# The last two graphs of a four-layer graph network on one core: parts of the final elu moved from ACT to DVE

## The chip, the cores and the metric

The kernel runs on 1 core of one Trainium2 chip. The metric is the device time of the program on that core in microseconds (us), taken as the median over several runs; lower is better. TensorE is called PE here, VectorE DVE, ScalarE ACT, GpSimd POOL and SyncE SP. Times written as 281.12 or the like are microseconds from the start of the profiled span.

## The reference, cut to what matters

There are 32 graphs of 256 nodes with 128 features each. Four layers run one after another, each with a residual sum around it. In all of them the input of the layer is normalised and rectified first.

```python
h = jnp.maximum(_layernorm(x, axis=-1), 0.0)
x = x + _L0_gnn_ref(h, adj, L0_gnn_W, L0_gnn_a)               # attention
h = jnp.maximum(_layernorm(x, axis=-1), 0.0)
x = x + _L1_gnn_ref(h, adj, L1_gnn_a0, L1_gnn_a1, L1_gnn_a2, L1_gnn_a3)
h = jnp.maximum(_layernorm(x, axis=-1), 0.0)
x = x + _L2_gnn_ref(h, L2_gnn_adj, adj, L2_gnn_weight, L2_gnn_bias)
h = jnp.maximum(_layernorm(x, axis=-1), 0.0)
x = x + _L3_gnn_ref(h, adj, L3_gnn_W, L3_gnn_a)
```

The last layer is the one that matters here: it ends with `jax.nn.elu(attention @ Wh)`, and the output is `x + elu(y)`, where y is the attended sum of a node divided by its softmax sum, and elu(y) is y for y > 0 and exp(y) - 1 otherwise.

## The kernel before, in words

A unit is one layer of one graph: 4 x 32 = 128 units, numbered n = 0 to 127 by the list `ORDER` (lines 37 to 42). The second half of the graphs ends the list, so units 112 to 127 are layer 3 of graphs 16 to 31, in order. A graph has its 256 nodes as 128 partitions times T = 2 rows each, so a tile of features is 128x256 numbers, or two of 128x128.

Every engine runs its own hand-ordered software pipeline (`pipeline`, lines 79 to 84). A list names stages with a lag and the layers for which they run; in step s a stage with lag L handles unit s - L, and the stages of a step are issued in the order of the list. An engine issues in program order, and semaphores bind the engines. What sets the order at the end, for the units of layer 3:

- PE, `put_o` (lag 8, line 972): the attended sums of a unit into a PSUM bank (lines 998 and 1001). It waits for a bank of three that ACT has read (`y_ready`, line 977).
- DVE, `invert_sums` (lag 11, line 704): the softmax sums are bounded below (line 710) and inverted (line 712) into `rinv`.
- ACT, `elu_parts` (lag 9, line 560): for each of the two halves t it writes exp(y) into `expy` (line 567) and max(y, 0) into `relu_y` (line 568), both read from the PSUM bank with `rinv` as the scale, so 4 instructions a graph; the last signals `y_ready`.
- DVE, `elu` (lag 13, line 732): `expy` becomes min(exp(y), 1) + max(y, 0) in one instruction (line 736), which signals `elu_ready`. That is elu(y) + 1; the 1 has been taken off before, since the residual x in `x1` was made with `bias_less_1` (lines 364 and 395).
- The sum `result` = `expy` + `x1`: for even graphs on POOL in `add_x_even` (lag 13, line 399), for odd graphs on DVE in `add_x` (lag 15, line 739). Each signals its half of `result_ready`.
- SP, `store` (lag 13, line 322): waits for `result_ready` of the graph, then issues its DMA of 128 KB to `out`, in the order of the graphs.

In a step of DVE's list `add_x` stands ahead of `take_rows`, `invert_sums` and `elu` (lines 749 to 751). So the end of DVE's program, with units named by their graph, runs: add_x(27), invert_sums(31), elu(29), elu(30), add_x(29), elu(31), add_x(31), as the even graphs have no instruction in `add_x`.

After that DVE collects a flag that says whether a general fallback must run: lines 757 and 761, a matmul of PE (line 1011), and line 763. All engines load the flag and branch on it. SP does so only when its waits for the last stores are over (line 329), then waits for the flag (line 331) and loads it (line 332). The program ends when every engine has gone past that branch.

Of the kernel before, what the change touches and what calls it, by code (L numbers as in the profile page):

```python
# [8 lines left out]
B, N, D = 32, 256, 128  # L9
P = 128  # L10
T = N // P
# [12 lines left out]


SLOTS = 8
BEHIND = 2
EARLY = 3
HS = 12
XS = 12  # L30
WIDE = 16
ROUNDS = B // SLOTS

ALL, ATTEND, GATS, NORMED, MULTI_REL, RGCN_REL = (0, 1, 2, 3), (0, 1, 3), (0, 3), (1, 2), (1,), (2,)
NOT_LAST, FIRST, LAST = (0, 1, 2), (0,), (3,)
# [14 lines left out]
def nth(layers, n):  # L50

    return COUNTS[layers][n]
# [21 lines left out]
def gat_slot(n):  # L74

    return (nth(GATS, n) - 1) % SLOTS

# [22 lines left out]
def gat_stack(nc, x, adj, w0, a0, m0, m1, m2, m3, w2, b2, w3, a3, out):  # L100
    f32, bf16, i32, u32 = mybir.dt.float32, mybir.dt.bfloat16, mybir.dt.int32, mybir.dt.uint32
    ALU = mybir.AluOpType
    ACT = mybir.ActivationFunctionType
# [7 lines left out]
    with ctx:  # L111
# [3 lines left out]
        def sem(name):  # L115
            return ctx.enter_context(nc.semaphore(name))
# [18 lines left out]
        x1 = sb("x1", [P, WIDE, T, D])  # L135
        edges = sb("edges", [P, SLOTS, T, N], i32)
        absent = sb("absent", [P, WIDE, T, N], bf16)

        h = sb("h", [P, HS, T, 1 + D])
        xb = sb("xb", [P, SLOTS, T, D])  # L140
        result = sb("result", [P, SLOTS, T, D])
        st = sb("st", [P, WIDE, T, 9])
# [4 lines left out]
        rinv = sb("rinv", [P, WIDE, T])  # L147

        hT = sb("hT", [P, 4, N])
        haT = sb("haT", [P, 4, N])  # L150
        val = sb("val", [P, SLOTS, T, D + 3])
        edgesT = sb("edgesT", [P, WIDE, T, N])
# [5 lines left out]
        relu_y = sb("relu_y", [P, 4, T, D])  # L158
        expy = sb("expy", [P, 4, T, D])
# [59 lines left out]
        def bank_o(n):  # L219
            return bank[O_BANK[n]][:, 0:T * (1 + D)].rearrange("p (t c) -> p t c", t=T)  # L220
# [4 lines left out]
        stored = [sem(f"stored{k}") for k in range(SLOTS)]  # L225
# [32 lines left out]
        sums_ready = sem("sums_ready")  # L258
        rinv_ready = sem("rinv_ready")
        elu_ready = sem("elu_ready")  # L260
        o_taken = sem("o_taken")
        xb_ready = sem("xb_ready")
        bias_ready = sem("bias_ready")
        result_ready = [sem("result_ready_even"), sem("result_ready_odd")]
# [28 lines left out]
        @block.sync  # L293
        def _(sp):

            def load_first(k):
                sp.dma_start(edges[:, k].rearrange("p t n -> p (t n)"), adj_v[k]).then_inc(edges_loaded[k], 16)

            for k in range(XS):
                sp.dma_start(xin[:, k].rearrange("p t d -> p (t d)"), x_v[k]).then_inc(x_loaded[k], 16)  # L300
                if 1 <= k <= SLOTS:
                    load_first(k - 1)
                if k == 2:
                    sp.dma_start(w_gat[1][:, 0:D], w3).then_inc(gat_loaded[1], 16)
                    sp.dma_start(a_gat[1][:, :], a3.rearrange("(c p) o -> p (c o)", c=2), allow_slow_non_contiguous=True).then_inc(gat_loaded[1], 16)
            for r, m in enumerate((m0, m1, m2, m3)):
                sp.dma_start(a_rel[:, r:r + 1], m.rearrange("(p o) -> p o", o=1)).then_inc(loaded, 16)
            sp.dma_start(w_rel[:, :, :], w2.rearrange("r i o -> i r o")).then_inc(loaded, 16)
            sp.dma_start(bias[:, :], b2.rearrange("(o d) -> o d", o=1).to_broadcast([P, D])).then_inc(loaded, 16)

            def load_x(n, layer, g):
                if g + XS < B:
                    sp.wait_ge(o_taken, nth(NOT_LAST, n))
                    sp.dma_start(xin[:, g % XS].rearrange("p t d -> p (t d)"), x_v[g + XS]).then_inc(x_loaded[g % XS], 16)

            def load_edges(n, layer, g):
                k = g % SLOTS
                if g + SLOTS < B:
                    sp.wait_ge(absent_ready, nth(FIRST, n))
                    sp.dma_start(edges[:, k].rearrange("p t n -> p (t n)"), adj_v[g + SLOTS]).then_inc(edges_loaded[k], 16)  # L320

            def store(n, layer, g):
                k = g % SLOTS
                sp.wait_ge(result_ready[g % 2], (nth(LAST, n) + 1) // 2)
                sp.dma_start(out_v[g], result[:, k].rearrange("p t d -> p (t d)")).then_inc(stored[k], 16)

            pipeline([(load_x, SP_LAG, FIRST), (load_edges, SP_LAG, FIRST), (store, SP_LAG + 1, LAST)])
            for k in range(SLOTS):
                sp.wait_ge(stored[k], 16 * ROUNDS)

            sp.wait_ge(flag_ready, 1)
            with sp.If(sp.value_load(flag[0:1, 0:1], min_val=0, max_val=P) > 0):
                sp.sem_inc(g_step, 1)
                sp.sem_inc(g_stored, 16)
                with sp.Fori(0, B) as g:

                    sp.wait_ge(g_step, g * G + 1)
                    sp.dma_start(gx[:, :, :].rearrange("p t d -> p (t d)"), x_v[bass.ds(g, 1), :, :].rearrange("o p n -> (o p) n")).then_inc(g_loaded, 16)
                    sp.dma_start(gadj[:, :, :].rearrange("p t n -> p (t n)"), adj_v[bass.ds(g, 1), :, :].rearrange("o p n -> (o p) n")).then_inc(g_loaded, 16)
                    sp.wait_ge(g_step, g * G + G + 1)  # L340
                    sp.dma_start(out_v[bass.ds(g, 1), :, :].rearrange("o p n -> (o p) n"), gout[:, :, :].rearrange("p t d -> p (t d)")).then_inc(g_stored, 16)
                sp.wait_ge(g_stored, 16 * B + 16)

        @block.gpsimd
        def _(pool):
# [52 lines left out]

            def add_x_even(n, layer, g):
                k = g % SLOTS  # L400
                if g % 2 == 0:
                    pool.wait_ge(elu_ready, nth(LAST, n))
                    if g >= SLOTS:
                        pool.wait_ge(stored[k], 16 * (g // SLOTS))
                    pool.tensor_tensor(result[:, k], expy[:, (nth(LAST, n) - 1) % 4], x1[:, g % WIDE], ALU.add).then_inc(result_ready[0], 1)
# [21 lines left out]
        def _(act):  # L427
# [132 lines left out]
            def elu_parts(n, layer, g):  # L560
                k = g % SLOTS

                act.wait_ge(rinv_ready, nth(ATTEND, n))
                if nth(LAST, n) > 4:
                    act.wait_ge(result_ready[g % 2], (nth(LAST, n) - 3) // 2)
                for t in range(T):
                    act.activation(expy[:, (nth(LAST, n) - 1) % 4, t], bank_o(n)[:, t, 0:D], ACT.Exp, scale=rinv[:, n % WIDE, t:t + 1])  # L567
                    last = act.activation(relu_y[:, (nth(LAST, n) - 1) % 4, t], bank_o(n)[:, t, 0:D], ACT.Relu, scale=rinv[:, n % WIDE, t:t + 1])  # L568
                last.then_inc(y_ready, 1)

            pipeline([(upper_part, 6, MULTI_REL), (scale_v, 6, LAST), (take_hT, 4, FIRST),
# [29 lines left out]
        def _(dve):  # L601
# [130 lines left out]
            def elu(n, layer, g):  # L732
                k = g % SLOTS

                dve.wait_ge(y_ready, nth(LAST, n))
                dve.scalar_tensor_tensor(expy[:, (nth(LAST, n) - 1) % 4], expy[:, (nth(LAST, n) - 1) % 4], 1.0, relu_y[:, (nth(LAST, n) - 1) % 4], ALU.min,  # L736
                                         ALU.add).then_inc(elu_ready, 1)

            def add_x(n, layer, g):
                k = g % SLOTS  # L740
                if g % 2 == 1:
                    dve.wait_ge(elu_ready, nth(LAST, n))
                    if g >= SLOTS:
                        dve.wait_ge(stored[k], 16 * (g // SLOTS))
                    dve.tensor_tensor(result[:, k], expy[:, (nth(LAST, n) - 1) % 4], x1[:, g % WIDE], ALU.add).then_inc(result_ready[1], 1)
# [21 lines left out]
            with dve.If(dve.value_load(flag[0:1, 0:1], min_val=0, max_val=P) > 0):  # L767
                with dve.Fori(0, B) as g:
# [6 lines left out]
                    for t in range(T):  # L775
                        last = dve.tensor_scalar(cols(gabsent, t), adj_t[:, t], 0.0, -BIG, ALU.is_le, ALU.mult)
                    last.then_inc(g_step, 1)
                    for t in range(T):
                        last = dve.tensor_scalar(cols(grel, t), adj_t[:, t], 0.0, float(R + 1), ALU.max, ALU.min)
# [6 lines left out]
                    for layer in range(4):  # L786
                        turn(g, f"{layer}stats")
                        for t in range(T):
                            last = dve.bn_stats(gst[:, t, :], gx[:, t, :])
# [3 lines left out]
                        for t in range(T):  # L793
                            last = dve.bn_aggr(gmv[:, t, :], gst[:, t, :])
                        last.then_inc(g_step, 1)
                        turn(g, f"{layer}norm")
                        for t in range(T):
                            last = dve.tensor_scalar(gxn[:, t, :], gx[:, t, :], gmv[:, t, 0:1], grs[:, t:t + 1],
                                                     ALU.subtract, ALU.mult)
# [14 lines left out]
                        if layer == 2:  # L814
# [5 lines left out]
                            for t in range(T):  # L820
                                last = dve.tensor_tensor(gxb[:, t, :], gx[:, t, :], bias[:, :], ALU.add)
# [3 lines left out]
                        else:  # L825
# [4 lines left out]
                            for t in range(T):  # L830
                                last = dve.scalar_tensor_tensor(gx[:, t, :], ps_o[:, t, :], grinv[:, t:t + 1],
                                                                gx[:, t, :], ALU.mult, ALU.add)
# [3 lines left out]
                    for t in range(T):  # L836
                        last = dve.tensor_scalar(gy[:, t, :], ps_o[:, t, :], grinv[:, t:t + 1], None, ALU.mult)
# [266 lines left out]
```

## Time and profile before

| what | us |
|---|---|
| median of 3 runs | 288.91 |
| lowest and highest of them | 288.39, 289.55 |
| the profiled execution, its own time | 288.16 |
| its span | 286.3 |
| outside the span | 1.86 |

The profile is of one execution. Busy time is given for each engine and line of the program; the timeline lists instructions with start and duration; the chain of waits follows the work that ended last back from the end. The profiled execution is 0.75 us shorter than the median of the runs.

### The profile page before, as it was taken

How to read it: one execution, taken by the hardware profiler on the slowest of the kernel's cores; microseconds unless marked ns; L12 is line 12 of the kernel's file. 1: busy time of each engine (PE TensorE's matmuls, PEld its weight loads, DVE VectorE, ACT ScalarE, POOL GpSimd, SP SyncE). 2: the span in 40 equal slices, each digit the busy share in tenths (PEclk: the TensorE clock that was granted, in tenths of full speed). 3: DMA queues.
4: the chain of work that ended last, by engine and by line, in shares of the span. 5: the costliest groups of instructions: out<-in, count | busy, mean ns of one | idle time of the engine just before them, and what ended most of it. 6: DMA issues, size and time to landing. Idle time of an engine off the chain costs nothing.

```text
span 286.3 us, 8109 instructions
## 1 busy us (share of the span) xinstructions
PE 273.2 (95%) x2250; PEld 256.9 (90%) x2250; DVE 252.1 (88%) x1217; ACT 255.4 (89%) x850; POOL 233.8 (82%) x376
## 2 busy tenths in 40 slices
PE   3899999999999999999999999999999999998991
PEld 1899998888889999999999999889889999998991
DVE  4799999988878887899999999998898888799985
ACT  5998988799998888999999999799999888796994
POOL 4899787777747999999999988887755799999722
PEclk9999999999999999999999999999999999999997
DMA  6955553400000000015343201000000000001213
GB/s 192 339 143 163 175 170 121 156 14 2 0 0 3 0 2 2 3 37 150 95 111 113 73 22 41 19 18 2 1 2 1 3 0 0 3 3 54 76 57 112
DMA packets 15949, 17.77 MB, mean 62 GB/s; under 512 B 2720, under 2 KB 11808, under 8 KB 15904
## 3 DMA queue, kind: packets, MB, share of 16 engines
q1 hardware_dynamic: 15488, 17.18, 19.2%
q8 instruction: 19, 0.31, 0.5%
q14 instruction: 26, 0.21, 0.2%
q10 hardware_dynamic: 416, 0.07, 0.1%
HBM read 13.05 MB, written 4.19 MB: 60 GB/s over the span
## 4 chain that ended last, share of the span: by engine, by line
PE 75%; DVE 14%; ACT 4%; issue 2%; POOL 2%; DMA 1%; SPq 1%; DVEq 0%
PE bank L1001 23%; PE bank L943 10%; PE bank L948 9%; PE bank L919 7%; PE bank L877 6%; PE bank L986 5%; PE bank L968 5%; DVE pT L700 4%; PE bank L956 4%; PE bank L998 3%; PE bank L950 2%; DVE st L625 2%; PE bank L903 2%; DVE mv L636 2%; DVE expy L736 1%
## 5 line engine op out<-in xcount | busy, mean ns | idle before, releaser
L367 POOL TENSOR_TENSOR rs<-mv,minus_half 128x2 f32<-128x2 f32 x128 | 89.7, 701 | 36.3 <-DVE mv L636 35.8
L1001 PE MATMUL bank<-val,pT 128*128 128x129 f32 x512 | 74.6, 275 | 0.0
L1001 PEld LDWEIGHTS bank<-val,pT 128*128 128x128 f32 x512 | 67.4, 192 | 0.0
L384 POOL TENSOR_TENSOR h<-h,rs 128x256 f32<-128x256 f32 x93 | 58.1, 625 | 2.3
L700 DVE SCALAR_TENSOR_TENSOR pT<-bank,val,edgesT 128x256 f32<-128x256 f32 x128 | 55.0, 471 | 0.8 <-PE bank L956 0.7
L625 DVE BATCH_NORM_STATS2 st<-x 128x6 f32<-128x128 f32 x192 | 45.2, 276 | 0.0
L528 ACT ACTIVATE val<-bank,val 128x128 f32<-128x128 f32 x128 | 44.3, 437 | 0.1
L636 DVE BATCH_NORM_AGGREGATE mv<-st 128x2 f32<-128x9 f32 x256 | 33.5, 172 | 10.8 <-DVE st L625 1.0
L877 PE MATMUL bank<-ident,h 128*128 128x128 f32 x192 | 38.0, 280 | 2.6 <-ACT hT L496 1.1
L376 POOL TENSOR_TENSOR h<-x,mv 128x256 f32<-128x256 f32 x64 | 40.0, 626 | 0.0
L919 PE MATMUL bank<-w_gat,hT 128*128 128x131 f32 x256 | 40.0, 279 | 0.0
L948 PE MATMUL bank<-hT,haT 128*128 128x256 f32 x128 | 36.7, 382 | 0.2 <-DVE pT L700 0.2
L998 PE MATMUL bank<-ident,vsum 128*128 128x128 f32 x128 | 35.0, 274 | 0.0
L919 PEld LDWEIGHTS bank<-w_gat,hT 128*128 128x128 f32 x256 | 34.3, 194 | 0.0
L1001 PE MATMUL bank<-h,pT 128*128 128x129 f32 x256 | 34.0, 275 | 0.1
L551 ACT ACTIVATE prob<-neg_s,neg_max 128x256 f32<-128x256 f32 x64 | 29.4, 516 | 5.1 <-DVE neg_max L684 5.0
L943 PE MATMUL bank<-edgesT,h 128*128 128x256 f32 x128 | 32.9, 380 | 0.0
L1001 PEld LDWEIGHTS bank<-h,pT 128*128 128x128 f32 x256 | 31.3, 191 | 0.5 <-issue 0.3
L567 ACT ACTIVATE expy<-bank,rinv 128x128 f32<-128x128 f32 x64 | 29.1, 470 | 2.8 <-DVE rinv L712 2.7
L684 DVE CUSTOM_DVE_ANT_0 neg_s<-bank,upper 128x256 f32<-128x256 f32 x64 | 24.6, 422 | 7.0 <-ACT upper L546 6.4
L496 ACT ACTIVATE hT<-bank 128x256 f32<-128x256 f32 x64 | 27.9, 436 | 2.9 <-PE bank L877 2.7
L568 ACT ACTIVATE relu_y<-bank,rinv 128x128 f32<-128x128 f32 x64 | 29.5, 477 | 0.0
(85 smaller groups left out, 661.0 us busy)
## 6 DMA issues: line engine op xcount, KB each, us to landing
edges<-in_adj SPq DMA_DIRECT2D x32, 256.0 KB, 3.0
xin<-in_x SPq DMA_DIRECT2D x32, 128.0 KB, 2.6
out_x<-result SPq DMA_DIRECT2D x32, 128.0 KB, 1.7
w_rel<-in_L_gnn_weight SPq DMA_DIRECT2D x1, 256.0 KB, 3.0
w_gat<-in_L_gnn_W ACTq DMA_DIRECT2D x1, 64.0 KB, 2.7
w_gat<-in_L_gnn_W SPq DMA_DIRECT2D x1, 64.0 KB, 3.4
a_rel<-in_L_gnn_a SPq DMA_DIRECT2D x4, 0.5 KB, 3.5
bias<-in_L_gnn_bias SPq DMA_DIRECT2D x1, 64.0 KB, 3.2
```

The source lines that it names most:

```text
L367: pool.tensor_tensor(rs[:, n % WIDE], mv[:, n % WIDE, :, 1], minus_half[:, :], ALU.pow).then_inc(rs_ready, 1)
L376: pool.tensor_tensor(h[:, n % HS, :, 0:D], xin[:, g % XS] if layer == 0 else x1[:, g % WIDE], mv[:, n % WIDE, :, 0:1].to_broadcast([P, T, ...
L384: pool.tensor_tensor(h[:, n % HS, :, 0:D], h[:, n % HS, :, 0:D], rs[:, n % WIDE, :].rearrange("p (t o) -> p t o", o=1).to_broadcast([P, T, ...
L528: last = act.activation(val[:, n % SLOTS, t, 0:D], bank_v(n)[:, t, 0:D], ACT.Copy, scale=val[:, n % SLOTS, t, D:D + 1])
L625: last = dve.bn_stats(st[:, n % WIDE, t, 0:6], src[:, t])
L700: last = dve.scalar_tensor_tensor(pT[:, n % 4, u], bank_z(n)[:, 0], val[:, n % SLOTS, u, D + 2:D + 3], edgesT[:, g % WIDE, u], ALU.max, AL ...
L877: last = pe.transpose(bank_x(n)[:, t * P:(t + 1) * P], h[:, n % HS, t, 0:D], ident[:, :])
L919: last = pe.matmul(bank_v(n)[:, t], hT[:, n % 4, t * P:(t + 1) * P], w_gat[layer // 3][:, 0:D + 3], start=True, stop=True)
L943: last = pe.matmul(z[:, 0], h[:, n % HS, u, 0:D], edgesT[:, g % WIDE, u], start=(u == 0), stop=(u == T - 1))
L948: pe.matmul(z[:, t], haT[:, n % 4, t * P:(t + 1) * P], hT[:, n % 4], start=True, stop=False, skip_group_check=True)
L998: pe.matmul(bank_o(n)[:, t, 0:D], vsum[:, gat_slot(n):gat_slot(n) + 1].to_broadcast([P, P]), ident[:, :], start=True, stop=False, is_trans ...
L1001: last = pe.matmul(bank_o(n)[:, t], pT[:, n % 4, u, t * P:(t + 1) * P], values[:, u], start=(u == 0 and layer == 1), stop=(u == T - 1), sk ...
```

## The change

For the graphs 30 and 31 (`LATE = 2`) ACT writes only the exponentials, 2 instructions a graph. DVE makes the rest in `elu`: one instruction over 128x256 turns exp(y) into min(exp(y), 1) - 1; after a wait for it, two instructions of 128x128 read y from the PSUM bank, scale it by `rinv`, and take the maximum with it, into `relu_y`, which now is elu(y). `add_x` then makes `result` = `relu_y` + 1 + `x1` on DVE for both graphs. POOL has no sum for graph 30 any more, and SP waits for a semaphore of its own, `late_ready`, before these two stores. By the order of the list the end of DVE's program becomes: add_x(27), invert_sums(31), elu(29), elu(30) with three instructions, add_x(29), elu(31) with three, add_x(30), add_x(31).

```diff
--- before.py
+++ after.py
@@ -24,6 +24,7 @@
 
 
 SLOTS = 8
+LATE = 2
 BEHIND = 2
 EARLY = 3
 HS = 12
@@ -258,6 +259,8 @@
         sums_ready = sem("sums_ready")
         rinv_ready = sem("rinv_ready")
         elu_ready = sem("elu_ready")
+        late_elu = sem("late_elu")
+        late_ready = sem("late_ready")
         o_taken = sem("o_taken")
         xb_ready = sem("xb_ready")
         bias_ready = sem("bias_ready")
@@ -321,7 +324,10 @@
 
             def store(n, layer, g):
                 k = g % SLOTS
-                sp.wait_ge(result_ready[g % 2], (nth(LAST, n) + 1) // 2)
+                if g < B - LATE:
+                    sp.wait_ge(result_ready[g % 2], (nth(LAST, n) + 1) // 2)
+                else:
+                    sp.wait_ge(late_ready, g - (B - LATE) + 1)
                 sp.dma_start(out_v[g], result[:, k].rearrange("p t d -> p (t d)")).then_inc(stored[k], 16)
 
             pipeline([(load_x, SP_LAG, FIRST), (load_edges, SP_LAG, FIRST), (store, SP_LAG + 1, LAST)])
@@ -398,7 +404,7 @@
 
             def add_x_even(n, layer, g):
                 k = g % SLOTS
-                if g % 2 == 0:
+                if g % 2 == 0 and g < B - LATE:
                     pool.wait_ge(elu_ready, nth(LAST, n))
                     if g >= SLOTS:
                         pool.wait_ge(stored[k], 16 * (g // SLOTS))
@@ -564,8 +570,9 @@
                 if nth(LAST, n) > 4:
                     act.wait_ge(result_ready[g % 2], (nth(LAST, n) - 3) // 2)
                 for t in range(T):
-                    act.activation(expy[:, (nth(LAST, n) - 1) % 4, t], bank_o(n)[:, t, 0:D], ACT.Exp, scale=rinv[:, n % WIDE, t:t + 1])
-                    last = act.activation(relu_y[:, (nth(LAST, n) - 1) % 4, t], bank_o(n)[:, t, 0:D], ACT.Relu, scale=rinv[:, n % WIDE, t:t + 1])
+                    last = act.activation(expy[:, (nth(LAST, n) - 1) % 4, t], bank_o(n)[:, t, 0:D], ACT.Exp, scale=rinv[:, n % WIDE, t:t + 1])
+                    if g < B - LATE:
+                        last = act.activation(relu_y[:, (nth(LAST, n) - 1) % 4, t], bank_o(n)[:, t, 0:D], ACT.Relu, scale=rinv[:, n % WIDE, t:t + 1])
                 last.then_inc(y_ready, 1)
 
             pipeline([(upper_part, 6, MULTI_REL), (scale_v, 6, LAST), (take_hT, 4, FIRST),
@@ -733,12 +740,26 @@
                 k = g % SLOTS
 
                 dve.wait_ge(y_ready, nth(LAST, n))
+                if g >= B - LATE:
+                    i = (nth(LAST, n) - 1) % 4
+                    dve.tensor_scalar(expy[:, i], expy[:, i], 1.0, -1.0, ALU.min, ALU.add).then_inc(elu_ready, 1)
+                    dve.wait_ge(elu_ready, nth(LAST, n))
+                    for t in range(T):
+                        last = dve.scalar_tensor_tensor(relu_y[:, i, t], bank_o(n)[:, t, 0:D], rinv[:, n % WIDE, t:t + 1],
+                                                        expy[:, i, t], ALU.mult, ALU.max)
+                    last.then_inc(late_elu, 1)
+                    return
                 dve.scalar_tensor_tensor(expy[:, (nth(LAST, n) - 1) % 4], expy[:, (nth(LAST, n) - 1) % 4], 1.0, relu_y[:, (nth(LAST, n) - 1) % 4], ALU.min,
                                          ALU.add).then_inc(elu_ready, 1)
 
             def add_x(n, layer, g):
                 k = g % SLOTS
-                if g % 2 == 1:
+                if g >= B - LATE:
+                    dve.wait_ge(late_elu, g - (B - LATE) + 1)
+                    dve.wait_ge(stored[k], 16 * (g // SLOTS))
+                    dve.scalar_tensor_tensor(result[:, k], relu_y[:, (nth(LAST, n) - 1) % 4], 1.0, x1[:, g % WIDE], ALU.add,
+                                             ALU.add).then_inc(late_ready, 1)
+                elif g % 2 == 1:
                     dve.wait_ge(elu_ready, nth(LAST, n))
                     if g >= SLOTS:
                         dve.wait_ge(stored[k], 16 * (g // SLOTS))
```

## Rows read from the trace of the kernel before

**Rows 1.** The page: busy us of each engine, with its share of the span.

```profile
PE 273.2 (95%) x2250; PEld 256.9 (90%) x2250; DVE 252.1 (88%) x1217; ACT 255.4 (89%) x850; POOL 233.8 (82%) x376
```

**Rows 2.** Chain of waits, its last stretch: start us, us, what.

```profile
282.14 0.60 DVE expy L736
...
282.76 0.43 DVE result L745
```

**Rows 3.** Timeline of PE, then ACT: start us, us, engine, line, tile, count.

```profile
279.70 0.61 PE L1001 MATMUL bank<-val,pT 128*128 128x129 f32 x4
...
279.91 0.39 ACT L567 ACTIVATE expy<-bank,rinv 128x128 f32<-128x128 f32 x1
...
280.91 0.42 ACT L567 ACTIVATE expy<-bank,rinv 128x128 f32<-128x128 f32 x1
...
281.66 0.45 ACT L568 ACTIVATE relu_y<-bank,rinv 128x128 f32<-128x128 f32 x1
```

**Rows 4.** Timeline of DVE's end; then line 736 from 281.05 to 281.5, ns minimum, median, maximum.

```profile
280.35 0.16 DVE L710 TENSOR_SCALAR sums<-bank 128x2 f32<-128x2 f32 x1
280.55 0.17 DVE L712 RECIPROCAL rinv<-sums 128x2 f32<-128x2 f32 x1
280.63 0.91 DVE L736 SCALAR_TENSOR_TENSOR expy<-expy,relu_y 128x256 f32<-128x256 f32 x2
281.45 0.42 DVE L745 TENSOR_TENSOR result<-expy,x 128x256 f32<-128x256 f32 x1
...
L736 DVE SCALAR_TENSOR_TENSOR expy<-expy,relu_y x2: 426/460/493, 280.6 to 281.1; 128x256 f32<-128x256 f32 x2
```

**Rows 5.** Timeline of POOL's end.

```profile
280.00 0.84 POOL L405 TENSOR_TENSOR result<-expy,x 128x256 f32<-128x256 f32 x1 [1.61 <-DVE expy L736]
281.61 0.83 POOL L405 TENSOR_TENSOR result<-expy,x 128x256 f32<-128x256 f32 x1 [0.78 <-DVE expy L736]
```

**Rows 6.** SP's two last stores, its wait for them, the drains that end SP and DVE.

```profile
282.48 0.33 SPq L325 DMA_DIRECT2D out_x<-result  x1
...
283.22 0.33 SPq L325 DMA_DIRECT2D out_x<-result  x1
...
L329 SPq EVENT_SEMAPHORE  x3: 27/28/28, 283.6 to 284.9; - x3
...
L111 DVEq DRAIN  x1: 45/45/45, 285.6 to 285.6; - x1
L111 SPq DRAIN  x1: 7/7/7, 286.1 to 286.1; - x1
```

**Rows 7.** Timeline of DVE elsewhere: the forms of the new instructions, and what follows them.

```profile
179.89 0.25 DVE L650 TENSOR_SCALAR h<-h 128x256 f32<-128x256 f32 x1
180.05 0.60 DVE L728 SCALAR_TENSOR_TENSOR x<-bank,rinv,xin 128x128 f32<-128x128 f32 x2
180.57 0.87 DVE L700 SCALAR_TENSOR_TENSOR pT<-bank,val,edgesT 128x256 f32<-128x256 f32 x2
...
279.51 0.41 DVE L736 SCALAR_TENSOR_TENSOR expy<-expy,relu_y 128x256 f32<-128x256 f32 x1
279.84 0.42 DVE L745 TENSOR_TENSOR result<-expy,x 128x256 f32<-128x256 f32 x1
```

**Rows 8.** Line 325, pairs of stores close together: near 263, then near 274.

```profile
L325 SPq DMA_DIRECT2D out_x<-result x2: 332/382/431, 263.1 to 263.4; - x2
...
DMA to landing us min/median/max: 2.3/2.3/2.3
...
L325 SPq DMA_DIRECT2D out_x<-result x2: 332/388/445, 273.9 to 274.5; - x2
...
DMA to landing us min/median/max: 1.8/1.9/1.9
```

**Rows 9.** Timeline of DVE and POOL near 258: a long instruction of line 736.

```profile
257.36 2.36 DVE L736 SCALAR_TENSOR_TENSOR expy<-expy,relu_y 128x256 f32<-128x256 f32 x1
...
258.81 0.62 POOL L376 TENSOR_TENSOR h<-x,mv 128x256 f32<-128x256 f32 x1
```

## The prediction

> **What bounds the kernel now.** The page comes first [rows 1]: PE is busy 95% of the span, and for most of it the kernel is bound by PE. The change touches none of that. It alters only the work of units 126 and 127 behind their matmuls, so I read the end: what happens between PE's last matmul and the end of the span. PE's last attended sum ends at 279.70 + 0.61 = 280.31 [rows 3]. Nothing in the change lets PE end sooner, since no later unit needs the banks that these two free.
>
> The chain of waits says what follows [rows 2]: ACT's halves of the elu, then line 736 (0.60), then line 745 (0.43), which ends at 283.19. The timeline shows ACT at work without a gap [rows 3]: graph 30 starts at 279.91, graph 31 at 280.91, and the last instruction ends at 281.66 + 0.45 = 282.11. The reader is to see that ACT takes about 0.26 for each instruction of 128x128, four a graph, and that graph 31 waits about 0.2 behind graph 30, since its rinv was ready at 280.55 + 0.17 = 280.72 [rows 4]. ACT is the bound of this stretch, and DVE is not: after 281.87 DVE stands still until 282.14.
>
> Behind 283.19 everything follows in lockstep [rows 6]. SP issues the last store at 283.22, has it landed at 284.9, loads the flag and drains at 286.1; DVE's flag path drains at 285.6, 0.5 earlier, although it starts from the same instruction. So the end is the last result plus 3.1, by way of the store, and the flag path has 0.5 to spare.
>
> **The change part by part.** All of it is added up as a new timeline. Durations are of one execution, whose own time of 288.16 lies 0.75 below the median; I carry the difference over to the median.
>
> ACT: four instructions of 0.26 go, 1.04 us. Graph 30 ends near 280.55. Graph 31 now has to wait for rinv at 280.72 and ends after two instructions, 280.74 + 0.26 + 0.37 = 281.37, which is 0.74 earlier than 282.11. That is what the change can give at most on ACT's side.
>
> POOL: one sum of 0.83 goes [rows 5]. It ran beside DVE and off the chain, but line 736 for graph 31 overlapped it and took 0.60 where it takes 0.41 alone [rows 2, 5, 7]. The likely loss of about 0.19 goes too. The sum of graph 28 (280.00 to 280.84) stays, and so does the 0.49 of line 736 for graph 29 beside it [rows 4, 5].
>
> DVE: what is the new instructions' price? None of them is in the trace by its line, but each form is [rows 7]. One over 128x256 with two constants in SBUF is like line 650: 0.25 (its other instances reach 0.31 at most). The pair from PSUM with a scalar pointer and a second tensor is like line 728: 0.60 for both, the next starting 0.52 after the first. I take that and keep line 700 (0.87 for two, but of 256 columns) as the upper end, 0.27 more a pair. The last sum, now a scalar_tensor_tensor over 128x256, is like line 736: 0.41; the old one had 0.42. An instruction that needs nothing starts 0.08 before the end of the one ahead (279.84 against 279.51 + 0.41). One that needs the result of the one ahead starts about 0.03 after its end (280.35 + 0.16 = 280.51, then 280.55 [rows 4]).
>
> In the program's order, with those numbers: rinv of graph 31 at 280.55, as before. Line 736 for graph 29: 280.63 to 281.12. Graph 30: the new instruction 281.04 to 281.29, its pair 281.32 to 281.92. The sum of graph 29, which stands behind them: 281.84 to 282.26 (before: 281.45 to 281.87 [rows 4]). Graph 31, whose exponentials have lain there since 281.37: 282.18 to 282.43, its pair 282.46 to 283.06. The sum of graph 30: 282.98 to 283.39. The sum of graph 31: 283.31 to 283.72, against 283.19. **DVE becomes the bound and the last result is 0.53 later.** DVE no longer waits for ACT; it is behind by 0.8 when graph 31 comes.
>
> SP: the waits for stores 30 and 31 change only their semaphore. Store 30 is issued at 283.42 and holds SP for 0.33, so store 31 follows at about 283.79, 0.57 later than 283.22. Before, these two were 0.74 apart [rows 6]; now they are 0.37 apart. How long does the second take to land? Alone it is 1.7 (283.22 to 284.9). A pair some 0.4 apart near 263 took 2.3 each, a pair 0.6 apart near 274 took 1.8 to 1.9 [rows 8]. The 2.3 is the nearer spacing, but its first store took 2.3 as well with nothing close ahead of it, so I do not put it all down to the spacing. I take 1.85, so 0.15 more, and keep 0 and 0.6 as ends.
>
> The wait of `add_x` for an earlier store of the slot costs nothing: those of graphs 22 and 23 landed several microseconds before. PE, the loads and all units before 126 are as they were, at no cost. The flag path moves by 0.53 and keeps its slack.
>
> The sum: 0.57 + 0.15 = 0.7. In the execution's own time 288.16 becomes 288.9, its span 286.3 becomes 287.0; against the median 288.91 becomes **289.6**.
>
> One rule of the Trainium skill would change this sum. The rows show that an instruction which waits for its predecessor starts 0.11 later than one that does not, and this happens twice on DVE's path, 0.22 in all [rows 4, 7]. By "VectorE: DVE Perf Modes", section "The DRAIN you can't avoid", the pipe empties after each instruction anyway and "the semaphore costs nothing extra here". With that, the sum would be 0.22 smaller, 289.4. The rows speak against it, and I go by them.
>
> **The rivals.**
>
> ACT's microsecond arrives (faster). If DVE had room, graph 31 would start at 281.40: 0.25, then the pair 281.68 to 282.28, then its sum 282.31 to 282.72, and the last result comes 0.47 earlier: 288.4. For it speaks that DVE idles 0.27 before 282.14 and that ACT ended the chain. Against it: the three instructions of graph 30 and two sums stand ahead in program order, and by the timeline above they don't fit. It needs DVE at graph 31 by 281.4, 0.8 sooner than I find. Chance 0.10.
>
> The pair of stores is the cost (slower, but inside what can be told). Everything as forecast, but 2.3 to land: 0.57 + 0.60 = 1.2, so 290.1. Chance 0.12.
>
> A stall on DVE beside POOL (slower, beyond doubt). Near 258 one instruction of line 736 took 2.36 instead of 0.41 while POOL ran one SBUF instruction after another [rows 9], and in the tail it took 0.60 beside one. If one of the eight late instructions met that, 1.95 would come on top of 0.7: 291.6. It decides from the point where POOL still works behind 281.04. Against it: POOL's last instruction now ends at 280.84. Chance 0.05. The page "SBUF — State Buffer" of the Trainium skill, section "SBUF: two separate sides", gives as the reason an exclusive lock that DVE and GpSimd share for a whole instruction; the 2.36 agrees with a lock that is lost several times over.
>
> The self-waits cost nothing (the rule above): 289.4, chance 0.08. The forecast itself has 0.65. That the change doesn't do what it says can't be: the relus and POOL's sum are gone from the program.
>
> **How the numbers follow.** A measurement of this kernel can tell about 0.5% from no change, 1.44 us. Forecast and three rivals lie between -0.5 and +1.2, all inside that bound. The range goes from the faster rival, 288.4, to the upper rival with the two pairs of line 728's form 0.4 dearer in all than I took them (their upper end is 0.54), 290.5. Outside are the stall (0.05) and chance shifts of a median of runs that lie 1.16 apart. Slower by more than 0.5% means above 290.35: the stall, and half of the 0.12 for the stores with an unlucky median: 0.11. Faster by more than 0.5% means below 287.47: a third of the faster rival by such a shift: 0.03. The rest, 0.86, is no change that can be told.
>
> **What would show it.** In the changed profile ACT's last instruction should end near 281.4, and the chain should run through DVE alone from rinv of graph 31 on, without a gap above 0.05. The line for the pair should show about 0.34 a piece with 0.26 between starts, the constant one 0.25. The last two stores should be some 0.37 apart, the second landing 1.7 to 2.3 after its issue. PE's last attended sum should end at 280.3 as before. The prediction is wrong if DVE idles ahead of graph 31, if the last result comes before 283.2, or if the pairs cost near 0.8.

## The result, and the profile after

The changed kernel is slower by 0.6%: ratio of the runs 1.0059, 95% interval 1.0035 to 1.0083. Its median is 290.7 us (288.82 to 291.48, 9 runs) beside 288.62 (288.01 to 290.17, 9 runs) for the kernel before. The same file timed again beside 35 runs of the kernel before gave 1.003 (1.0008 to 1.0052): median 288.93 against 288.33. The profiled execution took 290.9, its span 289.0. The forecast was 0.7 us more, 289.6. The sign was right, the size of the first measurement was not, and 290.7 lies just above the range's end of 290.5.

The page after (the columns are as in [rows 1]):

```profile
PE 275.4 (95%) x2250; PEld 259.2 (90%) x2250; DVE 252.9 (87%) x1222; ACT 254.9 (88%) x846; POOL 233.2 (81%) x375
```

The change is there: DVE has 5 instructions more, ACT 4 fewer, POOL one fewer. But the span grew by 2.7, more than any of that. PE's last attended sum says where. Line 1001 is 1022 now, and this row answers to the first of [rows 3]. It is from the timeline of PE.

```profile
281.69 0.61 PE L1022 MATMUL bank<-val,pT 128*128 128x129 f32 x4
```

It ends at 282.30, where it ended at 280.31. So 2.0 us went before PE's end, in a part that the change doesn't touch, and 0.7 behind it (289.0 - 282.30 = 6.70, was 286.3 - 280.31 = 5.99). I take the two apart.

**The end.** The timeline of DVE, then of ACT, answering to [rows 4] and [rows 3]:

```profile
282.53 0.17 DVE L719 RECIPROCAL rinv<-sums 128x2 f32<-128x2 f32 x1
282.62 0.49 DVE L752 SCALAR_TENSOR_TENSOR expy<-expy,relu_y 128x256 f32<-128x256 f32 x1
283.02 0.28 DVE L745 TENSOR_SCALAR expy<-expy 128x256 f32<-128x256 f32 x1
283.34 0.61 DVE L748 SCALAR_TENSOR_TENSOR relu_y<-bank,rinv,expy 128x128 f32<-128x128 f32 x2
283.87 0.41 DVE L766 TENSOR_TENSOR result<-expy,x 128x256 f32<-128x256 f32 x1
284.20 0.28 DVE L745 TENSOR_SCALAR expy<-expy 128x256 f32<-128x256 f32 x1
284.52 0.61 DVE L748 SCALAR_TENSOR_TENSOR relu_y<-bank,rinv,expy 128x128 f32<-128x128 f32 x2
285.05 0.75 DVE L760 SCALAR_TENSOR_TENSOR result<-relu_y,x 128x256 f32<-128x256 f32 x2
...
282.73 0.63 ACT L573 ACTIVATE expy<-bank,rinv 128x128 f32<-128x128 f32 x2 [0.19 <-DVE rinv L719]
```

ACT is done at 283.36, DVE takes graph 31 up at 284.20: 0.84 behind, where I had forecast 0.8. No row of DVE shows idle time. The last result comes at 285.80, which is 3.50 behind PE's last sum instead of 2.88 (283.19 - 280.31), so 0.62 later; 0.53 was forecast. SP's part, line 325 now being 331 and line 329 being 335, with the drains of [rows 6]:

```profile
L331 SPq DMA_DIRECT2D out_x<-result x2: 332/382/432, 285.5 to 285.9; - x2
...
DMA to landing us min/median/max: 1.7/1.8/1.8
...
L335 SPq EVENT_SEMAPHORE  x3: 28/28/28, 286.4 to 287.7; - x3
...
L112 DVEq DRAIN  x1: 44/44/44, 288.2 to 288.2; - x1
L112 SPq DRAIN  x1: 7/7/7, 288.8 to 288.8; - x1
```

The stores are some 0.4 apart, as forecast, and land in 1.8, not 2.3. SP still drains last.

**The start.** The timeline of the kernel before, DVE and PE, between 7 and 12 us. These rows were not read for the forecast:

```profile
7.55 0.49 DVE L625 BATCH_NORM_STATS2 st<-xin 128x6 f32<-128x128 f32 x2 [0.28 <-DMA xin<-in_x]
...
7.87 1.08 PE L919 MATMUL bank<-w_gat,hT 128*128 128x131 f32 x4
...
9.60 0.77 PE L919 MATMUL bank<-w_gat,hT 128*128 128x131 f32 x4
...
11.53 0.61 PE L919 MATMUL bank<-w_gat,hT 128*128 128x131 f32 x4
```

The same instructions in the changed kernel, whose lines are 632 and 940, with the issue of the load that DVE waits for and the instruction of DVE behind it:

```profile
4.02 0.47 SPq L303 DMA_DIRECT2D xin<-in_x  x1
...
8.60 0.49 DVE L632 BATCH_NORM_STATS2 st<-xin 128x6 f32<-128x128 f32 x2 [1.57 <-DMA xin<-in_x]
...
9.42 0.56 DVE L650 TENSOR_SCALAR h<-xin,mv,rs 128x128 f32<-128x128 f32 x2
...
10.13 0.66 PE L898 MATMUL bank<-ident,h 128*128 128x128 f32 x2 [0.99 <-DVE h L650]
10.58 1.08 PE L940 MATMUL bank<-w_gat,hT 128*128 128x131 f32 x4
...
13.05 1.08 PE L940 MATMUL bank<-w_gat,hT 128*128 128x131 f32 x4
...
15.42 0.96 PE L940 MATMUL bank<-w_gat,hT 128*128 128x131 f32 x4
```

Two things are to be seen. The x of the fourth graph, issued at 4.02 in both kernels, landed at 8.58 instead of 7.53 (DVE waits 1.57 for it). In DVE's program the statistics of the fourth graph stand ahead of `h` of the third (line 650), so PE waits 0.99 for the third graph, whose own x has long landed. And PE runs its four matmuls in 1.08 until past 15 us, where the kernel before has them in 0.61 from 11.5 on. That is a factor of two between starts (0.22 and 0.11 for one), the pace of the 1.2 and the 2.4 GHz level. The column of the granted clock says 1.00 for both kernels in this stretch, so only the durations show it; that they are these two levels is read from the factor. Together they cost 2.3 by 18 us, of which 0.35 is made good later. The instructions up to here are the same in both programs. Is it chance, or does the changed program bring it about?

### The profile page after: what moved, and what is told of

Same layout as the page of the kernel before. It is cut to its first block, busy times and chain, and to the rows that moved or that the text cites. A ratio compares the mean times of both kernels' runs of the same rounds, so it can differ in the third digit from the quotient of the medians.

```text
span 289.0 us, 8109 instructions
## 1 busy us (share of the span) xinstructions
PE 275.4 (95%) x2250; PEld 259.2 (90%) x2250; DVE 252.9 (87%) x1222; ACT 254.9 (88%) x846; POOL 233.2 (81%) x375
## 4 chain that ended last, share of the span: by engine, by line
PE 86%; DVE 8%; DMA 2%; ACT 1%; SPq 1%; issue 1%; DVEq 0%
PE bank L1022 27%; PE bank L964 10%; PE bank L940 9%; PE bank L969 9%; PE bank L898 7%; PE bank L977 5%; PE bank L1007 5%; PE bank L989 5%; PE bank L1019 4%; PE bank L924 2%; PE bank L971 2%; DVE pT L707 2%; DMA xin<-in_x 2%; PE bank L943 1%; DVE expy L752 1%; DVE st L632 1%
## 5 line engine op out<-in xcount | busy, mean ns | idle before, releaser
L940 PE MATMUL bank<-w_gat,hT 128*128 128x131 f32 x256 | 41.1, 285 | 0.0
L940 PEld LDWEIGHTS bank<-w_gat,hT 128*128 128x128 f32 x256 | 35.4, 200 | 0.0
L575 ACT ACTIVATE relu_y<-bank,rinv 128x128 f32<-128x128 f32 x60 | 27.8, 480 | 0.0
```

The lines of the kernel that those rows point to most:

```text
L940: last = pe.matmul(bank_v(n)[:, t], hT[:, n % 4, t * P:(t + 1) * P], w_gat[layer // 3][:, 0:D + 3], start=True, stop=True)
```

## The experiments

The theories: **S**, the start scatters by itself, in both kernels, and the change costs only what lies behind PE's end; **P**, the slow start belongs to the changed program. For the end: DVE's queue is the bound, against the form of the instructions or the shared use with POOL.

**same_before and same_after**: the two kernels unchanged.

> The kernel before, unchanged, timed against itself. Both theories agree on the stretch behind PE's last attended sum: 6.0 us to the end of the span, as in the profile of before (286.3 - 280.3). Theory S (the start scatters by itself): a good part of the runs, between a tenth and a half, lie some 1.5 to 2.3 us above the rest, as 3 of the 9 runs of before did. Theory P (the slow start belongs to the changed program): hardly any of these do. The ratio to the kernel before should be 1 within 0.3%.

> The changed kernel once more. Both theories: 6.7 us from the end of PE's last attended sum to the end of the span. Theory S: slow and quick starts mix about as in the kernel before, and the median settles at 0.7 above it (ratio 1.0025), or up to 1.5 above where the draw of starts is unlucky. Theory P: most runs start slowly again, as 7 of 9 did, and the ratio stays at 1.006 or more, with the profile's time lost before 20 us.

Measured: same_before 288.01 (12 runs, 287.78 to 290.19), ratio 0.9992 (0.9971 to 1.0013), and same_after 288.93 (12 runs, 288.52 to 290.76), ratio 1.003. Of the changed kernel's first 9 runs 7 lay over 1.2 us above the lowest, now 3 of 12; of the kernel before it was 3 of 9, and now 2 of 12 of the copy. The profiled executions swapped roles: same_before had the slow start, same_after the quick one. The timeline of PE in same_before:

```profile
10.78 1.08 PE L919 MATMUL bank<-w_gat,hT 128*128 128x131 f32 x4
...
13.26 1.08 PE L919 MATMUL bank<-w_gat,hT 128*128 128x131 f32 x4
```

and in same_after:

```profile
10.03 1.08 PE L940 MATMUL bank<-w_gat,hT 128*128 128x131 f32 x4
...
12.03 0.61 PE L940 MATMUL bank<-w_gat,hT 128*128 128x131 f32 x4
```

PE's last sum ends at 282.36 in same_before and at 280.38 in same_after. The lowest runs of these two series differ by 0.74 (288.52 and 287.78); the 35 runs of the kernel before go down to 287.27, so a lowest run is a weak ruler. P falls as far as it ties the slow start to the changed program: both programs have both starts, and of the 35 runs of the kernel before 15 lie over 1.2 us above the lowest. Whether the change makes the slow start somewhat more frequent (10 of 21 runs against 20 of 56) these runs can't tell. The stretches behind PE's end are 5.94 and 6.72, as forecast.

All profiles, taken from the chain and the timelines (us; the second column is how long after its issue at 4.02 the x of the fourth graph landed):

| kernel | landed after | PE's last sum ends | last result behind it | span's end behind it |
|---|---|---|---|---|
| before | 3.51 | 280.31 | 2.88 | 5.99 |
| same_before | 4.77 | 282.36 | 2.87 | 5.94 |
| after | 4.56 | 282.30 | 3.50 | 6.70 |
| same_after | 4.01 | 280.38 | 3.50 | 6.72 |
| late1 | 4.49 | 281.24 | 3.37 | 6.46 |
| halves | 3.82 | 280.47 | 2.93 | 6.03 |
| no_self_wait | 3.56 | 280.11 | 3.24 | 6.49 |
| sum30_on_pool | 3.35 | 280.26 | 3.81 | 6.94 |
| relu_first | 3.56 | 279.96 | 2.47 | 5.74 |

PE's end follows the landing: up to 4.01 it is at 280.0 to 280.5, from 4.4 on at 281.2 to 282.4. The landing isn't all of it: late1 and the changed kernel have it at 4.49 and 4.56 and are 1.06 apart, since PE's four matmuls are down to 0.61 at 14.75 in late1 and still take 0.96 at 15.42 in the other. The time behind PE's end is the same with either start to 0.05, in both kernels that were seen with both, and that is the ruler for what follows.

**late1**: `LATE = 1` in place of 2.

> Only graph 31 is taken over by DVE; graph 30 is made as before, with its sum on POOL. By my timeline DVE begins graph 31 at 281.8 and ends its sum 0.05 before the time of the kernel before: 5.9 to 6.0 us behind PE's last attended sum, if DVE's new instructions aren't held up by POOL's sum of graph 30 that runs beside them. If the two engines exclude each other, the one-source instruction or the last sum waits up to 0.6, and the stretch is up to 6.6. The rival that DVE's queue is not the cost but the form of the new instructions expects half of the loss, 6.35.

Measured: last result 3.37 behind PE's end, span's end 6.46 behind; the runs 288.86, ratio 1.002 (0.9995 to 1.0044). The timeline of DVE, then of POOL:

```profile
282.70 0.81 DVE L745 TENSOR_SCALAR expy<-expy 128x256 f32<-128x256 f32 x1
...
282.52 0.84 POOL L411 TENSOR_TENSOR result<-expy,x 128x256 f32<-128x256 f32 x1 [0.76 <-DVE expy L752]
```

The instruction that takes 0.28 in the changed kernel takes 0.81 here, and ends 0.15 after POOL's sum. The 0.53 is the whole difference to my 2.83. So DVE's instruction is held up by POOL's, as the expectation's middle branch had it; the form of the instructions is not the cost.

**halves**: the kernel before, with the elu of graph 31 in two steps.

```diff
+                    if g == B - 1 and t == 0:
+                        last.then_inc(y_half, 1)
...
+                if g == B - 1:
+                    dve.wait_ge(y_half, 1)
+                    dve.scalar_tensor_tensor(expy[:, i, 0], expy[:, i, 0], 1.0, relu_y[:, i, 0], ALU.min, ALU.add).then_inc(elu_half, 1)
+                    dve.wait_ge(y_ready, nth(LAST, n))
+                    dve.scalar_tensor_tensor(expy[:, i, 1], expy[:, i, 1], 1.0, relu_y[:, i, 1], ALU.min, ALU.add).then_inc(elu_ready, 1)
+                    return
```

> The kernel before with the elu of graph 31 alone taken in two halves: DVE makes the first half while ACT still works on the second, so only 128 columns stand behind ACT's last instruction. If ACT is the bound of the old end, 0.27 + 0.42 follow ACT instead of 0.60 + 0.43, and the stretch behind PE's last attended sum is 5.6 to 5.7 instead of 6.0. If DVE's fixed cost for an instruction eats it: 6.0.

Measured: 2.93 and 6.03, no gain; ratio 1.0002 (0.9979 to 1.0025). Neither branch named the cause. DVE's timeline and POOL's:

```profile
281.94 0.81 DVE L742 SCALAR_TENSOR_TENSOR expy<-expy,relu_y 128x128 f32<-128x128 f32 x1
282.67 0.28 DVE L744 SCALAR_TENSOR_TENSOR expy<-expy,relu_y 128x128 f32<-128x128 f32 x1
...
281.76 0.84 POOL L407 TENSOR_TENSOR result<-expy,x 128x256 f32<-128x256 f32 x1 [0.77 <-DVE expy L747]
```

The first half, meant to run while ACT works, stands behind POOL's sum until 282.75 and ends 0.15 after it, like in late1.

**no_self_wait and sum30_on_pool** start from the changed kernel. Both leave out a part of the arithmetic, as told in their expectations, and each is read from one profiled execution.

```diff
-                    dve.tensor_scalar(expy[:, i], expy[:, i], 1.0, -1.0, ALU.min, ALU.add).then_inc(elu_ready, 1)
-                    dve.wait_ge(elu_ready, nth(LAST, n))
+                    dve.tensor_scalar(spare[:, i], expy[:, i], 1.0, -1.0, ALU.min, ALU.add).then_inc(elu_ready, 1)
```

> The changed kernel with its first new instruction writing to a spare tile, so that the pair behind it needs no wait for it. The pair reads the raw exponentials: the output of graphs 30 and 31 leaves out the min and the - 1. By the rows, a self-wait costs 0.11 each, 0.22 for both, and the last result of DVE comes 3.3 us behind PE's last attended sum instead of 3.5. By the rule that a semaphore costs nothing extra behind the pipe's drain: 3.5, no change.

Measured: 3.24. DVE's timeline:

```profile
281.89 0.28 DVE L746 TENSOR_SCALAR spare<-expy 128x256 f32<-128x256 f32 x1
282.09 0.59 DVE L748 SCALAR_TENSOR_TENSOR relu_y<-bank,rinv,expy 128x128 f32<-128x128 f32 x2
```

The pair starts 0.20 after the instruction ahead of it, against 0.32 with the wait (284.20 to 284.52). The two waits cost 3.50 - 3.24 = 0.26.

```diff
+                if g == B - LATE:
+                    pool.wait_ge(late_elu, 1)
+                    pool.wait_ge(stored[k], 16 * (g // SLOTS))
+                    pool.tensor_tensor(result[:, k], relu_y[:, (nth(LAST, n) - 1) % 4], x1[:, g % WIDE], ALU.add).then_inc(pool_late, 1)
```

> The changed kernel with the sum of graph 30 on POOL; the + 1 of graph 30 is left out. If DVE's queue is the bound of the new end, the last result comes 0.33 earlier (3.15 to 3.2 behind PE's last attended sum), unless POOL, which would then run beside DVE's instructions for graph 31, holds DVE up: by what late1 and halves showed (0.81 instead of 0.27) an instruction of DVE that starts inside POOL's 0.84 ends about 0.15 after POOL does. POOL would begin some 0.1 after the pair of graph 30 and cover the sum of graph 29 and the first instruction of graph 31, so the net should be 3.2 to 3.6, and the instruction that is held up should be seen at 0.6 or more.

Measured: 3.81, 0.2 beyond my range. DVE is rid of one sum of 0.33, and yet the end is 0.31 later. The timelines of DVE and POOL:

```profile
282.17 0.81 DVE L750 TENSOR_SCALAR expy<-expy 128x256 f32<-128x256 f32 x1
283.01 0.61 DVE L753 SCALAR_TENSOR_TENSOR relu_y<-bank,rinv,expy 128x128 f32<-128x128 f32 x2
283.65 0.42 DVE L767 SCALAR_TENSOR_TENSOR result<-relu_y,x 128x256 f32<-128x256 f32 x1
...
281.99 0.83 POOL L411 TENSOR_TENSOR result<-relu_y,x 128x256 f32<-128x256 f32 x1 [1.21 <-DVE relu_y L753]
```

0.53 is lost behind POOL, and 0.11 since the sum of graph 31 now follows directly on the pair that it needs; -0.33 + 0.53 + 0.11 = 0.31.

**relu_first**: what these say together. ACT ended the old chain, DVE had two dependent instructions behind it, and POOL stood in DVE's way. So for graphs 30 and 31 ACT writes both relus first, DVE adds x to them while ACT makes the exponentials, and one instruction is left.

```diff
+                    dve.wait_ge(relu_ready, g - (B - LATE) + 1)
+                    dve.tensor_tensor(relu_y[:, i], relu_y[:, i], x1[:, g % WIDE], ALU.add).then_inc(relu_sum, 1)
...
+                    dve.wait_ge(y_ready, nth(LAST, n))
+                    dve.wait_ge(relu_sum, g - (B - LATE) + 1)
+                    dve.scalar_tensor_tensor(result[:, k], expy[:, i], 1.0, relu_y[:, i], ALU.min, ALU.add).then_inc(late_ready, 1)
```

> The kernel before with another split for graphs 30 and 31: ACT writes both relus first and then both exponentials, DVE adds the residual to the relus meanwhile, and only one instruction, min(exp, 1) + that sum, stands behind ACT. No sum of graph 30 on POOL. By my timeline the last result comes 2.45 to 2.5 behind PE's last attended sum instead of 2.9, and the end 5.5 to 5.6 behind it instead of 5.95. If the count of DVE's instructions alone decides, as in the changed kernel, it is 2.9 or more. In the median of runs 0.4 less than before, ratio 0.9985, hardly to be told.

Measured: last result 2.47 behind PE's end, as forecast, and the span's end 5.74, 0.15 more than forecast. The last store lands 1.8 after its issue instead of 1.7. That fits the closeness of the two: all kernels whose last two stores are some 0.4 apart have 1.8, all others 1.7. The runs: 288.1 against 288.25, ratio 0.9995 (0.9977 to 1.0013). By the profile it beats the kernel before by 0.2 to 0.25 and the changed one by 1.0; by the runs the first can't be told.

**warm_before, warm_after, warm_relu_first**: matmuls of the identity into an unused bank, 8 before PE's first wait, 4 around the first weights, 3 ahead of the second and third graph.

> The kernel before with 18 matmuls of the identity into an unused bank while PE waits for the first loads and between the first units. Theory S says that the upper runs come from a late load of x that leaves PE idle while it is still at its lower clock, so that PE stays there some 5 us longer. With PE busy from 2 us on the upper level (0.61 for the four matmuls of a graph's values instead of 1.08) should be there by 8 us in every run: quick starts gain 0.5 to 1 us, slow ones 1.5 to 2, median near 287.3, and the scatter narrows to under 1.5 us. If the clock has no part in it and the loads alone set the start: no change of the median beyond 0.3, and the same scatter.

> The changed kernel with the same 18 matmuls. The difference to warm_before should be the cost of the end by itself, 0.7 to 0.8, and no longer mixed with the start. If the change had a hand in the start: 1.5 or more.

> Both together, relus first and the warm PE. If the two effects add up: 0.4 below warm_before and 1.0 or more below the kernel before, median near 286.9 to 287.5. If the start gives nothing: 0.4 below the kernel before.

Measured: 290.6 (290.28 to 291.54), ratio 1.0083 (1.0062 to 1.0105); 291.83, ratio 1.0114 (1.0091 to 1.0137); 290.51, ratio 1.0074 (1.0055 to 1.0094); 6 runs each. All slower by over 2 us. At the start PE's pace did what theory S says, but the time did not follow as forecast. In warm_relu_first the load of x was late (4.51), and yet:

```profile
7.70 0.81 PE L955 MATMUL bank<-w_gat,hT 128*128 128x131 f32 x4
...
10.32 0.61 PE L955 MATMUL bank<-w_gat,hT 128*128 128x131 f32 x4
```

PE's last sum ends at 280.89 there. Without the warming it ended at 281.24 (late1), 282.30 and 282.36 with a late load, and near 280.0 with an early one. So of the 2 us of a slow start the late load by itself is about 0.9 (280.89 less 280.0, an estimate from single profiles), and PE's low pace the rest. With an early load the warming gained next to nothing: in warm_before the load landed after 3.51 as in the kernel before, and PE's last sum ends at 279.98 against 280.31 there and 279.96 in relu_first, which isn't warmed; 0.5 to 1 us was forecast. The chain of waits says why, in both alike:

```profile
8.53 0.70 POOL rs L367
...
9.30 0.61 POOL h L376
9.91 0.65 POOL rs L367
```

POOL's part of the normalisation sets a quick start between 8.5 and 13 us, not PE. The scatter of warm_before is 1.26 over 6 runs, that of same_before 2.41 over 12, which is too few to say that it narrowed. The end of warm_before is 8.5 behind PE's end instead of 5.95, though its last result comes 2.86 behind, as ever. These 2.5 us are the loss: without them its median would be 288.05, 0.2 under the 288.25 of the kernel before. The rows of the engines' branches over the fallback (minimum, median, maximum in ns), of PE in same_before and then in warm_before:

```profile
L1034 PEldq COMPARE_BRANCH  x1: 365/365/365, 287.0 to 287.0; - x1
```

```profile
L1043 PEldq COMPARE_BRANCH  x1: 3566/3566/3566, 284.6 to 284.6; - x1
```

The difference warm_after to warm_before is 1.23 in the medians, between my two cases; with 6 runs each and a scatter of 1.3 it doesn't decide. Their stretches from PE's end to the last result differ by 0.64 (3.50 and 2.86).

**relu_first_warm8 and relu_first_warm4**, to see what makes the branch long:

```diff
+            for _ in range(8):
+                pe.transpose(bank[7][:, 0:P], ident[:, :], ident[:, :])
```

> relu_first with 8 warming matmuls, all of them before PE's first wait, so 16 instructions of PE more instead of 36. The kernels with 18 matmuls lost 2.5 to 2.6 at their very end, where PE's branch over the fallback took 3.6 instead of 0.37. If that comes from where PE's program lies, it may be gone with fewer instructions (then the end is 5.75 behind PE's last attended sum and the median lies near 287.5 to 288.0), or still there (then 8.2 behind, median near 290.3). If it came from the warming itself (the clock, the unused bank), it is there in any case.

> The same with 4 warming matmuls, 8 instructions of PE more. By the place of the program the branch should be short here if it is short with 8 matmuls, and may be short where it is long with 8. With 0.9 us of matmuls before the first wait the clock should rise no later than without them; if it rises by 8 us as with 18, the median is 287.5 to 288.0, otherwise as relu_first, 288.1.

Measured: 290.56 (9 runs), ratio 1.0077 (1.0051 to 1.0102), and 289.38 (12 runs), ratio 1.0035 (1.0015 to 1.0055). The branch, with 8 and then with 4:

```profile
L1063 PEldq COMPARE_BRANCH  x1: 4046/4046/4046, 286.4 to 286.4; - x1
```

```profile
L1063 PEldq COMPARE_BRANCH  x1: 365/365/365, 285.5 to 285.5; - x1
```

Sixteen more instructions of PE bring the long branch, eight don't. The other runs agree: with 8 every span is 288.3 or more, with 4 the lowest is 285.6, as in relu_first. With 4 the end is 5.73 behind PE's end again, but the kernel is still not quick: its profiled execution took 289.95 at a span of 286.9, so 3.05 lie outside the span. It is 3.05 to 3.65 in all 12 of its runs, and 1.75 to 1.94 in every run of the other kernels. By the spans alone it is as quick as relu_first (medians 286.0 and 286.2, in series of their own). What happens outside the span no profile shows. Both had a late load (4.44), and neither raised PE's pace as early as 18 matmuls did: with 8 the four matmuls still took 1.08 at 12.93, with 4 they took 0.75 there. That fewer gave the higher pace sooner shows that the number of warming matmuls alone doesn't set it.

## Why the prediction was right or wrong

- **That the end is read from ACT's chain, and PE's end doesn't move for the change**: right. All three profiles with the old tail gave 2.86 to 2.88, all three with the changed one 3.50.
- **DVE becomes the bound; 0.8 behind at graph 31**: right, 0.84. ACT's microsecond ends in nothing, and the faster rival is out, since the three instructions of graph 30 and two sums stand ahead of graph 31.
- **The prices**: the pair 0.61 (forecast 0.60), the instruction with two constants 0.28 (0.25), the last sums as forecast. The whole from PE's end to the last result was 0.62 instead of 0.53, an error of 0.09, of which 0.08 come from the 0.03 and the 0.01, each of them twice.
- **The self-waits**: the rows had 0.11 each, the experiment shows 0.13. The rule of the Trainium skill ("VectorE: DVE Perf Modes", section "The DRAIN you can't avoid"), that the semaphore costs nothing extra, doesn't carry over to this pair of instructions. The figure there is from eight copies in a row, and the same section says that a next instruction which isn't held back starts earlier; the 0.20 between starts without the wait, against 0.32 with it, agrees with that. The rival built on it (289.4) is out.
- **The stores**: forecast 1.85 to land, measured 1.8. The rival with 2.3 did not occur in any of the profiles with close stores. The 2.3 near 263 is thus not the price of the spacing.
- **The stall beside POOL**: right that it can't happen in the changed kernel, and right as a mechanism. Where line 736, a half of it, or the new instruction with two constants starts inside POOL's sum, it ends 0.15 to 0.3 after POOL does, in late1, halves, sum30_on_pool and the old tail. That the change takes POOL's sum away is a gain within it: put back in sum30_on_pool, it costs 0.31 more, and late1, which keeps it, is only 0.13 better with half of DVE's new work.
- **The failed step is the one under "How the numbers follow"**: the scatter of a median was taken from three runs (1.16 from end to end) and given 0.1 or so on the upper side. The runs have a dense lower group and a tail that reaches 2 to 3 above the lowest, from the landing of the third x and PE's pace behind it, and a median of nine can fall into either. In the first measurement it fell into the tail for the changed kernel and into the lower group for the kernel before: 0.7 of the 2.1 between the medians is the change, the rest the draw. My sentence that all units before 126 are as they were was right as to the program and useless as to the time. Had I looked at the first 20 us, the 1.08 of PE's matmuls at 7.87 and DVE's wait of 0.28 for x would have hinted that the start can be a term. Its size one quick profile could not show: the slow start is 2.0 in the profiles of after and same_before.
- The point "no change that can be told" had 0.86. The first measurement gives 0.59%, the second 0.3%, the profiles 0.7 to 0.8 us, 0.26%. I hold to the last, as the only one that the draw of the start can't touch; with it, 289.6 was a good forecast for the change, and that 290.7 was measured first was bad luck with the draw.

What stays open: what makes the load issued at 4.02 land after 3.4 us in one execution and after 4.8 in another, why the share of slow starts was 7 of 9 in one series and 3 of 12 in the next, and what the 1.2 us outside the span of relu_first_warm4 are. A run that holds the loads of x fixed wasn't tried.

## What to carry to other kernels

Before work is moved from the engine that ends the chain to its neighbour, lay the neighbour's instructions out in program order with start-to-start times: 0.27 of idle time in front of the last item can't take 0.85 of new work for the item before it (283.02 to 283.87, and one sum more, less one instruction of the old kind). At the end of a program, look for what can be done ahead of the late operand (relus and residual first, exponentials last), which costs no instruction more in all, DVE having one from POOL. And time two kernels by a stretch of the profile that the start can't touch, since their medians may differ by the draw of the start alone.

## What the runs showed of the hardware that I had not expected

**Some DVE instructions that start inside one of POOL's wait for its end, others don't at all.** A DVE instruction of 0.28 that started inside POOL's sum of 0.84 took 0.81 and ended 0.15 after POOL, in late1, halves and sum30_on_pool. This agrees with the Trainium skill, "SBUF — State Buffer", section "SBUF: two separate sides", by which the second fully blocks when the DVE instruction is in a two-port mode or has two inputs in SBUF. Held up were the tensor_scalar with one source and the scalar_tensor_tensor with two. Not held up was the reciprocal of 128x2: it began at 280.55, inside POOL's sum of 280.00 to 280.84, and took its 0.17 [rows 4, 5]. The other order, POOL starting inside an instruction of DVE, was not tested.

**A branch at the end of PE's program took 0.37 or 3.6 to 4.0**, and went with how long PE's program ahead of it was: short with none or 4 matmuls added (8 instructions, each with its weight load), long with 8 or 18. The Trainium skill, "Runtime: NRT & Kernel Launch", section "Instruction fetch mechanics", has it that a taken branch whose target isn't in the pages at hand must wait for them to be fetched. That fits a step that comes with the place in the program, but that it is the cause was not tested apart. Here 16 to 36 instructions more at the start of PE's program went with an end that was 2.5 to 2.9 us later.

**PE's pace at the start depends on when the data comes.** A load 1 us later went with an end 2 us later, and PE then stayed at the pace of 1.2 GHz (0.22 for a matmul) until past 15 us. Where PE had 18 matmuls more in the first 9 us, it was at the pace of 2.4 GHz (0.11) by 10.3 in spite of the late load, and PE's last sum ended at 280.89, 0.9 behind a quick start; 8 early ones alone didn't do it. The granted clock of the profile stands at 1.00 in all of these stretches.
